# Masked cross-attention on one core: mixing steps and jobs put between the two score steps of a group, four value jobs moved to the start of the stage, and a seven-bank ring for the last ten groups

## The reference, cut to what matters

```python
x = x + _L3_xattn_ref(_layernorm(x, axis=-1), ctx_1024, mask_BxS2_ik0, L3_xattn_q_w, L3_xattn_q_b,
                      L3_xattn_k_w, L3_xattn_k_b, L3_xattn_v_w, L3_xattn_v_b)
```

## Time and profile before

| | us |
|---|---|
| Median of 3 runs | 1735.02 (1732.46 to 1739.79) |
| The profiled execution | 1739.7 |
| Its span, first to last instruction | 1737.9 |
| Granted TensorE clock, mean of the span | 0.949 |
| PE busy | 1551.3 (89%) |
| DVE busy | 799.9 (46%) |
| ACT busy | 630.3 (36%) |
| Maxima of DVE (line 1813), 256 of them, busy | 302.9 |

### The profile page before, as it was taken

One profiled execution on the slowest core, in us unless ns is written; L12 is line 12 of the kernel. 1 busy time (PEld: TensorE's weight loads), 2 busy tenths in 40 slices (PEclk: granted clock), 3 DMA queues, 4 the chain that ended last, 5 costly groups with the idle time before them and its releaser, 6 DMA issues.

```text
span 1737.9 us, 23533 instructions
## 1 busy us (share of the span) xinstructions
PE 1551.3 (89%) x9628; PEld 949.9 (55%) x9628; DVE 799.9 (46%) x1418; ACT 630.3 (36%) x1161; POOL 144.4 (8%) x181
## 2 busy tenths in 40 slices
PE   7998999999999989998898888888888888677698
PEld 3676544454676445685544344554444444544597
DVE  5543430013334234333523766666678843656432
ACT  1222321013333224324313456566566773203111
POOL 0001200001001110001103112002300000000000
PEclk9999999999999999999998899999999999877699
DMA  9033133200124100212323645345655305100050
GB/s 378 8 113 139 59 106 115 65 21 17 49 93 174 45 32 1 97 55 83 94 112 70 114 84 93 76 81 92 183 88 135 47 2 207 49 0 1 1 194 13
DMA packets 40402, 147.08 MB, mean 85 GB/s; under 512 B 6092, under 2 KB 21708, under 8 KB 30668
## 3 DMA queue, kind: packets, MB, share of 16 engines
q1 hardware_dynamic: 40296, 145.58, 29.5%
HBM read 122.99 MB, written 22.56 MB: 84 GB/s over the span
## 4 chain that ended last, share of the span: by engine, by line
PE 81%; DVE 8%; ACT 8%; issue 3%; DMA 0%; SPq 0%; DVEq 0%; ACTq 0%
PE PS L156 52%; PE PS L1796 8%; PE PS L1708 7%; PE PS L1694 2%; PE PS L558 2%; PE PS L1187 2%; ACT AR L1896 1%; ACT H L1896 1%; PE PS L1364 1%; ACT CT L1896 1%; DVE SM L1813 1%; PE PS L1197 1%; ACT CN L1410 1%; PE PS L2278 1%; PE PS L2214 1%
## 5 line engine op out<-in xcount | busy, mean ns | idle before, releaser
L1813 DVE TENSOR_REDUCE SM<-PS 128x1 f32<-128x1024 f32 x256 | 302.9, 1220 | 132.1 <-PE PS L1694 131.3
L1708 PE MATMUL PS<-AR 49*128 49x256 bf16 (+1 forms) x1216 | 171.6, 277 | 31.5 <-DVE AR L1834 10.6
L156 PE MATMUL PS<-CT,HT 128*128 128x512 f32 x416 | 190.4, 593 | 2.0 <-ACT HT L662 2.0
L156 PE MATMUL PS<-CN,AR 128*128 128x256 f32 (+1 forms) x832 | 188.0, 371 | 0.0
L156 PE MATMUL PS<-HT,AR 128*128 128x512 f32 x328 | 164.8, 656 | 15.0 <-ACT HT L330 10.2
L156 PEld LDWEIGHTS PS<-CN,AR 128*128 128x128 f32 x832 | 151.0, 190 | 44.0 <-issue 28.7
L1708 PE MATMUL PS<-AR,CT 49*128 49x256 bf16 (+1 forms) x832 | 129.2, 275 | 33.6 <-DVE AR L1834 10.6
L156 PE MATMUL PS<-AR 128*128 128x512 f32 (+3 forms) x472 | 144.1, 459 | 7.0 <-DVE AR L593 2.5
L156 PEld LDWEIGHTS PS<-HT,AR 128*128 128x128 f32 x328 | 66.5, 210 | 104.7 <-issue 101.8
L156 PEld LDWEIGHTS PS<-AR 128*128 128x128 f32 x472 | 83.1, 190 | 68.2 <-issue 50.7
L156 PEld LDWEIGHTS PS<-CT,HT 128*128 128x128 f32 x416 | 73.6, 190 | 71.0 <-issue 66.0
(11 more groups left out here) (302 smaller groups left out, 1997.1 us busy)
## 6 DMA issues: line engine op xcount, KB each, us to landing
CN<-ctx_n SPq DMA_DIRECT2D x24, 1024.0 KB, 4.8
AR<-k_parts SPq DMA_DIRECT2D x114, 128.0 KB
CT<-pack SPq DMA_DIRECT2D x7, 2048.0 KB, 7.3
k_parts<-CN SPq DMA_DIRECT2D x32, 384.0 KB, 3.4
CT<-k_parts SPq DMA_DIRECT2D x78, 128.0 KB
v_ones<-CN SPq DMA_DIRECT2D x32, 288.0 KB, 3.3
CN<-v_ones SPq DMA_DIRECT2D x8, 1152.0 KB, 8.9
CT<-ctx_t SPq DMA_DIRECT2D x8, 1024.0 KB, 19.1
```

Source lines behind the costliest of these rows:

```text
L156: last = te.matmul(o, l, r, start=first and k == 0, stop=final and k == n - 1, skip_group_check=True)
L1708: return te.matmul(PS[:, b, z * 256:z * 256 + 256], keys[rows, c * 128:c * 128 + 128], QQ9[rows, pr, rest, cols], start=not rest, stop=boo ...
L1813: ve.tensor_reduce(MX9[:, p % 2, e, g % 8 // 4, g % 4:g % 4 + 1], PS[:, b:b + 2, :].rearrange("p a b -> p (a b)"), AX, ALU.max).then_inc(* ...
```

## The change

In pair_steps() the step "score" of a group becomes two, "first" (step 2g, with the best products beside it) and "second" (step 2g + 1), and "mix" now stands for one step, not for two. In a group without a job the mix of step 2g - 2 comes between "first" and "second", that of step 2g - 1 after "second". In a group with a job the job comes between them, and both mixes follow "second". All engines walk the new order.

The jobs: four value jobs go from place "heads" to place "s9" (27 jobs in the loop become 23, and 6 in the start become 10). In the loop the jobs stood at k = 1, 3 and 5 of the first nine pairs; now they stand at k = 1, 3 and 5 of pairs 0 to 4 and at k = 1 and 4 of pairs 5 to 8. In the start the selects move from u = 0, 2, 6, 10 to u = 0, 4, 8, 12, and eight jobs follow the best products of u = 1, 3, ... 15 (before: four jobs, ahead of those of u = 3, 5, 7, 9).

The ring: score banks of the last ten groups come from LR9, a ring of seven banks (0 to 6), in place of SR9.

```diff
-                             ("b9", "vv"), ("s9", "kkkvvv"), ("heads", "kkv" * 4 + "v" * 7 + "k" * 8)):
+                             ("b9", "vv"), ("s9", "kkkvvvvvvv"), ("heads", "kkv" * 4 + "vvv" + "k" * 8)):
...
-        for n in range(27):
-            PAIR_JOBS[8 * (n // 3) + 2 * (n % 3) + 1] = jobs.pop(0)
+        for p in range(9):
+            for k in (1, 3, 5) if p < 5 else (1, 4):
+                PAIR_JOBS[8 * p + k] = jobs.pop(0)
...
             for u in range(2 * AHEAD):
-                if u in (0, 2, 6, 10):
-                    yield "select", (0, 2, 6, 10).index(u), 0
-                if u > 2 and u % 2 and jobs:
+                if u in (0, 4, 8, 12):
+                    yield "select", u // 4, 0
+                yield "best", u // 2, u % 2
+                if u % 2 and jobs:
                     yield ("job", *jobs.pop(0))
-                yield "best", u // 2, u % 2
...
             for g in range(128):
                 p, k = g // 8, g % 8
-                yield "score", g, 0
-                if g:
-                    yield "mix", g - 1, 0
+                yield "first", g, 0
                 if g in PAIR_JOBS:
                     yield ("job", *PAIR_JOBS[g])
+                elif g:
+                    yield "mix", 2 * g - 2, 0
+                yield "second", g, 0
+                if g in PAIR_JOBS:
+                    yield "mix", 2 * g - 2, 0
+                if g:
+                    yield "mix", 2 * g - 1, 0
                 if k == 2 and p:
                     yield "finish", p - 1, 0
...
-            yield "mix", 127, 0
+            yield "mix", 254, 0
+            yield "mix", 255, 0
             yield "finish", 15, 0
...
+        LR9 = banks.ring((0,), (1,), (2,), (3,), (4,), (5,), (6,))
...
             def score_bank(p, s, e):
-                b, before = SR9.take(("st", 9, p, s, e), ("e", 9, p, s, e))
+                ring = SR9 if 8 * p + s // 2 + AHEAD < 128 else LR9
+                b, before = ring.take(("st", 9, p, s, e), ("e", 9, p, s, e))
...
-                if what == "score":
+                if what == "first":
                     p, s = n // 8, 2 * (n % 8)
                     if n + AHEAD < 128:
                         best_beside(n + AHEAD, 0, p, s)
                         best_beside(n + AHEAD, 1, p, s)
                     else:
                         both(p, s)
-                    both(p, s + 1)
+                if what == "second":
+                    both(n // 8, 2 * (n % 8) + 1)
...
-                    first = 1 if n + AHEAD < 128 else 0
-                    exp(p, s, first)
-                    exp(p, s, 1 - first)
-                    exp(p, s + 1, 0)
-                    exp(p, s + 1, 1)
+                    e = 1 if n + AHEAD < 128 else 0
+                    exp(p, s, e)
+                    exp(p, s, 1 - e)
+                if what == "second":
+                    exp(n // 8, 2 * (n % 8) + 1, 0)
+                    exp(n // 8, 2 * (n % 8) + 1, 1)
```

More of the change, by code:

```diff
@@ L1788, in pe_9 @@
                 if what == "mix":
-                    p = n // 8
+                    p, s = n // 16, n % 16
                     b2, pr, _ = of_pair(p)
[L1791 to L1799, removed]
+                    pe.wait_ge(("e", 9, p, s, 0), ("e", 9, p, s, 1), ("cx", 9, p - 1) if p else None, ("v_in", b2, s // 4))
+                    for y in range(4):
+                        h = 2 * pr + y // 2
+                        z = te.matmul(PS[32 * y:32 * y + 32, 7, 0:256], VP9[:, 2 * s + y % 2, 17 * h:17 * h + 32],
+                                      PT9[n % 6][:, y, :], start=s == 0, stop=s == 15, skip_group_check=True)
+                    z.then_inc(*pe.inc("mixed", "mix", 9, p, s))
             pe.end(9)
@@ L1913, in act_9 @@
             for what, n, k in pair_steps():
-                if what == "score":
+                if what == "first":
                     p, s = n // 8, 2 * (n % 8)
-                    first = 1 if n + AHEAD < 128 else 0
-                    exp(p, s, first)
-                    exp(p, s, 1 - first)
-                    exp(p, s + 1, 0)
-                    exp(p, s + 1, 1)
+                    e = 1 if n + AHEAD < 128 else 0
[4 more added lines that the diff above has]
+                    exp(n // 8, 2 * (n % 8) + 1, 1)
                 if what == "job":
                     job_act(ac, n, k)
-                if what == "mix" and n % 8 == 7:
-                    p = n // 8
+                if what == "mix" and n % 16 == 15:
+                    p = n // 16
                     ac.wait_ge(("mix", 9, p, 15), ("fin_ps", 9, p - 2) if p > 1 else None)
@@ L1979, in sync_9 @@
             for what, n, k in pair_steps():
-                if what == "score" and n % 8 == 0:
+                if what == "first" and n % 8 == 0:
                     p = n // 8
@@ L1988, in sync_9 @@
                     job_sp(sp, n, k)
-                if what == "mix" and n // 8 == 7 and n % 2:
-                    q = n % 8 // 2
+                if what == "mix" and n // 16 == 7 and n % 4 == 3:
+                    q = n % 16 // 4
                     sp.wait_ge(("mix", 9, 7, 4 * q + 3), *[("stored", "v", j) for j in range(16, 32)])
@@ L1993, in sync_9 @@
                         *sp.lands(f"v_in{q}", "v_in", 1, q))
-                if what == "score" and n == 80:
+                if what == "first" and n == 80:
                     sp.wait_ge(("job_ps", "k", 31), ("job_ps", "v", 31))
```

## The result

Predicted 1690 us (1679 to 1710), faster with a chance of 93%. Measured: 1690.78 us, median of 4 runs (1688.6 to 1693.0), against 1737.4 for the kernel before (4 runs, 1732.46 to 1743.67). The ratio is 0.973, 95% interval 0.9693 to 0.9766: 47 us faster. The profiled execution has a span of 1689.5 us for 1737.9 before, 48.4 less. The profiled one of the four runs of experiment 5 was in a slower state (2626 us, at a mean granted clock of 0.55) and is left out of that experiment's numbers.

A forecast was written before the change was run, and what follows sets the result against it. PE's own order, with a bank wait in each plain group, was taken as the bound. Loop gain 46 plus last ten groups 5.5 less start 7 gave 45 us: 1695 us like the profiled execution, 1690 as median, range 1679 to 1710.

The forecast's parts named there:

- What bounds a plain group: Loop groups without a job: PE's own order with a bank wait; mix fills it, 2.97 to 2.69 us.
- Job group: Loop groups with a job: the job covers the hole, both mixes stay together, 4.90 to 4.46 us.
- Group k = 7: Second step waits for the turned rows' bank; one mix moves in front, 4.11 to 3.78 us.
- Loop in sum: Groups 2 to 117: 428.7 to 382.8 us, a gain of 46.
- the clock: Loop: five pair starts at 1.2 GHz cost 5.8 us; half of it was taken to remain.
- rival 2: DVE or ACT holds the plain group at about 2.85 us, 13 us less gain: 1703 us; 18%.
- Last ten groups: With seven banks PE's 2.24 us a group is left: 26.2 against 31.8 us, gain 5.5 (3 to 7).
- Start: Added jobs: ACT's copy waits for a value store behind key jobs, holding a select; 7 us lost (2 to 12).
- The sum: Whole kernel: 46 + 5.5 - 7 = 45 us gained; 1695 us like the profiled execution, 1690 as median.
- Shape changes at a higher price: Lone mix at 0.70 us makes a plain group 2.95 us, no gain there: 1713 us in all; 10%.
- Slower than before: Lone mix at 0.95 us makes plain groups 3.45 us, 61 us lost against the forecast: 1751 us; 2%.
- little effect: Something unrecorded holds PE, or the start loses over 30 us to stores: 1727 to 1743 us; 4%.

The follow-up runs named there:

- experiment 5: Changed kernel with DVE copying the turned rows ahead of both maxima at k = 7, not between them: 1681.56 us, median of 3 runs.
- experiment 1: Changed kernel with the jobs placed as before (6 in the start, 27 in the loop), new order and seven-bank ring kept: 1690.16 us.
- experiment 2: Changed kernel with jobs placed as before and the three-bank ring in the last ten groups too, so only the new order: 1692.98 us.
- experiment 3: Kernel before with only the seven-bank ring in the last ten groups, old order: 1737.15 us in one run, last ten groups 24.4 us.
- experiment 7: Changed kernel with SP's stores of the start in turn, key and value, not three keys first: 1681.17 us in one run, start 32.5 us.
- experiment 4: Changed kernel with both mixes of a group between first and second, none behind second: 1709.76 us in one run.
- experiment 6: Kernel before with DVE copying the turned rows ahead of both maxima at k = 7: 1722.72 us in one run.
- experiment 8: Changed kernel with turned rows copied first, start stores in turn, and both mixes behind second in the last ten groups: 1669.98 us.

## Why the prediction was right

**What bounds a plain group: right, and to the size.** The wait for the bank of the first exponential was the hole, and a lone mix fills it. The lone mix was taken at 0.57 us and took 0.57; the group came to 2.67, where I had 2.67 and added 0.02 for DVE. That addition was wrong in its size: DVE's second maximum ends 3.00 us into the group as computed, but the second best product's matmul starts 0.46 us into a group, not 0.35 (about there stands its weight load), so the handover just fits. Waits of PE for maxima come to 1.0 us in the whole loop.

**Job group: right.** 4.46 forecast, 4.46 measured. (Such a group has one change of shape more than before, not two, as the prediction says of each group; its pieces have it right.) **Group k = 7: 3.78 forecast, 3.67 measured;** the 0.1 for a late maximum wasn't paid, and PE's wait fell from 1.5 to 0.9 us. The group with turned rows took 0.06 longer than allowed for, 2.95 in place of 2.89.

**Loop in sum: 46 forecast, 52.4 measured.** The term that was mis-sized is the clock: I took half of its 5.8 us, and all of it came back (2.9 more). The rest: 80 x 0.02 for DVE, 14 x 0.1 at k = 7 and 1.5 for late exponentials that cost nothing, together 4.5, less 14 x 0.06 for the groups with turned rows and 0.6 where the statistics of x at the end of batch 0 stand on DVE; about 0.4 is left over and not assigned. The statistics I overlooked: group 67 took 3.18 us and group 68 5.15, for 2.67 and 4.46, since DVE has no slack left to hide 1.2 us of small work (0.6 of it stood in the kernel before too, and so in the forecast's small rest). It is the mechanism of rival 2, in one place of the loop, not in every group, and it hangs on where the jobs stand: in experiment 1, where group 67 has a job, the same work cost nothing. Experiment 2 shows that the order alone makes the loop this fast.

**Last ten groups: 5.5 forecast, 4.9 measured,** right in its cause. But the working put PE's 2.24 us "just above" a bound of ACT at 2.16, and ACT's four exponentials take about 2.0. So the old order with seven banks is faster there, and that part of the change loses 2.5 us against what the ring alone gives (experiment 3). In the expectation of experiment 2 I left out that the next first step waits for a bank of the second one: 1.39 us from one step to the other, as in the earlier trace rows, makes 2 x 1.39 = 2.78, and 2.76 was measured.

**Start: 7 lost forecast, 6.8 measured.** The step was that ACT's copy of the third value job waits for the first one's store, behind three key stores, and holds a select. That is what the trace shows, somewhat longer (PE idle for 5.2 us and not 4), while the select and the job behind it ran at half clock and the later ones at full. Experiment 7 removes the wait and with it the whole loss.

**The sum: closer than its terms.** The stretches gained 50.2 us where the forecast had 45, since the loop gave 6 more. Of these, 1.8 us went in the stages around. For an execution like the profiled one the forecast was 1695, and it took 1691.3. The forecast then took off 4.7 us, by which the profiled execution of the kernel before lay above the median; that of the changed kernel lay only 0.5 above its own. The two misses cancel, so that the median came within 1 us of 1690 is luck; the mechanisms are right without it.

**The rivals.** Shape changes at a higher price (10%) fell on the time line of the plain group, where the lone mix takes 0.57 us; experiment 3 prices them by the difference of two orders, 2.24 against 2.00 us for two more in a group, 0.12 each where I had 0.1. DVE or ACT as the bound of the plain group at 2.85 us (18%) fell on the same time line: 2.67 us, and 1.0 us of waits for maxima in the whole loop.

The Trainium skill, TensorEngine Tiling (Array Packing), Key Properties, states that changing the tiling mode drains TensorE; the traces agree that each change costs time, at 0.12 us. That is less than the 0.166 us which the prediction estimated from the Trainium skill, TensorE: Matmul & The Clock Gate, Single matmul latency.

Slower than before (2%) and little effect (4%) had no part in it. What would have been worth a rival of its own is that a part of the change gives nothing: the moved jobs are worth 0 (experiment 1), and become worth nearly 7 us only with SP's stores in turn (experiment 7).

## What to carry to other kernels

Where an engine waits for a ring of few buffers between two pieces of its own work, put work that is ready into that gap, and size the gain from one period of the time line: pieces, gaps and the hand-over back to the engine that is nearly full. Put it there only as long as the wait exists; with buffers to spare the same interleaving cost 0.24 us a group. When jobs are added ahead of a queue, follow each one to its store: here one store in the wrong place of an in-order queue cost as much as four jobs saved. Two copies, 0.6 us together, that DVE made between two maxima of 1.2 us each held PE for 1 us in every pair; the order on the helping engine is as much worth a look as that on the busy one.

## What the runs showed of the hardware that was not expected

- The granted clock in the loop fell to half (1.2 GHz) five times in the kernel before (pairs 0, 3, 6, 8 and 9) and five times in experiment 3 (pairs 4, 6, 10, 11 and 12), always behind the wait of 1.5 us at k = 7. Each of the two has 14 such waits; why these ten of the 28 and not the others is not shown. It never fell in the loop of the seven profiles in which this wait was 0.9 us or less (the changed kernel and experiments 1, 2, 4, 6, 7 and 8). With the waits of 0.37 us kept and only the long one removed (experiment 6) the clock stayed at 2.4 GHz.
- ACT's exponentials of 128 x 512, 0.6 us each, run about 0.5 us apart when four stand in a row, so twice the 1.08 us of a pair overstates four of them.
- The start of the stage took the same 32.5 us with six jobs at a mean clock of 0.76 (experiment 1, 32.65) and with ten jobs at 0.98 (experiment 7): more work for PE, at a higher clock, in the same time.
